# Last layer of a perceiver stack: four tiles in step, against two pairs of tiles half a pass apart

## What the last layer computes

```python
h = x + attention(rmsnorm(x, ln1_w), ...)     # x: layer-normed stream
out = h + moe(rmsnorm(h, ln2_w), ...)
# in moe:
probs = jax.nn.sigmoid(x @ router_w + router_b)
scores, idx = jax.lax.top_k(probs, TOPK)
for e in range(NR):
    combined = combined + w[..., e:e + 1] * expert_ffn(x, r_gate[e], r_up[e], r_down[e])
# expert_ffn: (silu(x @ wg) * (x @ wu) / SCALING) @ wd
# stream: x = x + _L3_ffn_ref(_layernorm(x), ...)
```

## Time and profile before

| | us |
|---|---|
| median of 3 runs (lowest, highest) | 4422.85 (4418.86, 4425.76) |
| the profiled execution's own time | 4422.6 |
| its span, first to last instruction | 4420.8 |
| last layer: first instruction of pass 0 to last of pass 1 | 4100.65 to 4414.15 |
| its two passes | 157.25 and 156.25 |

### The profile page before, as it was taken

How to read it: one execution, slowest core, us unless ns; L and a number is a source line. 1 busy time by engine, 2 the same in 40 slices (tenths; PEclk the granted TensorE clock), 3 DMA queues, 4 the chain that set the end, 5 groups by cost and what they waited for, 6 DMA issues and landing times. The chain is left out here.

```text
span 4420.8 us, 69997 instructions
## 1 busy us (share of the span) xinstructions
PE 3591.5 (81%) x26672; PEld 2566.4 (58%) x26672; DVE 2633.6 (60%) x5418; ACT 1722.9 (39%) x3305; POOL 361.6 (8%) x566
## 2 busy tenths in 40 slices
PE   7999998997787887753888776878888886878778
PEld 4655557876764555531555643535555555757667
DVE  6888885443367777876444363247667665453552
ACT  4888883111344343421333212224444442223323
POOL 3000000000000000000111000111111111121000
PEclk8555558998886666756988788989999997989787
DMA  2000001000010000010000014000000001200000
GB/s 78 1 0 0 0 0 72 0 0 19 7 36 20 0 0 0 0 58 2 5 5 5 5 59 134 0 3 3 3 5 3 3 3 35 82 0 0 1 1 10
DMA packets 44826, 72.66 MB, mean 16 GB/s; under 512 B 25805, under 2 KB 33489, under 8 KB 41045
## 3 DMA queue, kind: packets, MB, share of 16 engines
q1 hardware_dynamic: 36440, 70.54, 4.6%
q10 hardware_dynamic: 8256, 0.52, 0.2%
HBM read 67.91 MB, written 3.15 MB: 16 GB/s over the span
## 5 line engine op out<-in xcount | busy, mean ns | idle before, releaser
L1316 DVE TENSOR_SCALAR_CACHE_REDUCE l0x_ex<-l0x_s_ps 128x1024 f32<-128x1024 f32 x258 | 305.6, 1222 | 63.4 <-PE l0x_s_ps L1019 62.4
L1151 ACT ACTIVATE l0x_ex<-l0x_ex,l0x_neg_max,l0x_q_scale 128x2048 f32<-128x2048 f32 x128 | 267.9, 2093 | 52.4 <-DVE l0x_neg_max L1322 50.7
L1031 PEld LDWEIGHTS l0x_t_ps<-l0x_identb,l0x_pb 128*128 128x128 bf16 x2048 | 200.0, 142 | 109.4 <-issue 56.8
L1019 PE MATMUL l0x_s_ps<-l0x_kT,l0x_qT 64*128 64x512 bf16 x516 | 235.5, 600 | 32.9 <-ACT l0x_qT L1146 19.5
L1158 ACT ACTIVATE l0x_pt<-l0x_t_ps 128x1024 bf16<-128x1024 bf16 x256 | 246.3, 1014 | 32.2 <-PE l0x_t_ps L1031 32.2
L1031 PE MATMUL l0x_t_ps<-l0x_identb,l0x_pb 128*128 128x128 bf16 x2048 | 233.7, 304 | 6.8 <-ACT l0x_pt L1158 4.1
L1331 DVE TENSOR_SCALAR l0x_pb<-l0x_ex 128x2048 bf16<-128x2048 f32 x128 | 156.4, 1222 | 0.0
L263 PE MATMUL l3x_bank<-l3x_wproj,l3x_cat 128*128 128x256 f32 x512 | 120.7, 390 | 32.1 <-DVE l3x_cat L3345 32.1
L263 PE MATMUL l3x_bank<-l3x_w_kv_x,l3x_ctxT 128*128 128x512 f32 x256 | 129.8, 655 | 0.9 <-ACT l3x_ctx_q L762 0.9
L263 PEld LDWEIGHTS l3x_bank<-l3x_wproj,l3x_cat 128*128 128x128 f32 x512 | 96.1, 193 | 52.4 <-DVE l3x_cat L3345 38.7
L1019 PEld LDWEIGHTS l0x_s_ps<-l0x_kT,l0x_qT 64*128 64x128 bf16 x516 | 50.0, 121 | 129.4 <-issue 80.4
(11 more groups left out here) (740 smaller groups left out, 8651.6 us busy)
## 6 DMA issues: line engine op xcount, KB each, us to landing
l3x_wproj<-in_L_xattn_wproj SPq DMA_DIRECT2D x1, 4096.0 KB, 22.5
l3a_w<-in_L_attn_W SPq DMA_DIRECT2D x4, 1024.0 KB, 11.4
l2f_w<-in_L_ffn_w SPq DMA_DIRECT2D x1, 2816.0 KB, 12.4
l0x_ctxT<-in_ctxT SPq DMA_DIRECT2D x8, 256.0 KB, 3.0
l0a_wq<-in_L_attn_W_Q SPq DMA_DIRECT2D x1, 2048.0 KB
l0a_wk<-in_L_attn_W_K SPq DMA_DIRECT2D x1, 2048.0 KB
l0a_wv<-in_L_attn_W_V SPq DMA_DIRECT2D x1, 2048.0 KB, 8.0
l0a_wo<-in_L_attn_W_O SPq DMA_DIRECT2D x1, 2048.0 KB, 13.0
```

The costliest lines, as they stand in the source:

```text
L1019: ins = mm(s_ps[:, j * 512:(j + 1) * 512], qT[rows, h // 2, :], kT[rows, h // 2, j * 512:(j + 1) * 512], start=True, stop=True)
L1031: ins = nc.tensor.transpose(t_ps[:, j * P:(j + 1) * P], pb[:, h % 2, j * P:(j + 1) * P], identb[:])
L1151: s.activation(ex[:, h % 4, :], ex[:, h % 4, :], ACT.Exp, scale=q_scale[:, h:h + 1], bias=nb[:, h:h + 1], accum_out=sums[:, h:h + 1]).then ...
L1316: v.tensor_scalar(ex[:, h % 4, c], s_ps[:, c], 1.0, None, ALU.mult, ALU.max, accum_out=mx[:, h, half:half + 1]).then_inc(o.up(scores_taken ...
```

## The change

Within the pairs (0, 1) and (2, 3) the ways stay in step. The pairs are 16 steps apart: way n waits `16 * (n // 2)` empty steps in the order in which instructions are written. The loop over passes is unrolled, in Python: each way writes pass 1 directly behind its pass 0. The order has 80 rounds where there were 2 times 32: rounds 0 to 15 hold steps 0 to 15 of the first pair alone; rounds 16 to 63 hold, in each round, a step of the attention half of one pair and of the expert half of the other; rounds 64 to 79 hold steps 16 to 31 of the second pair alone. In a round the instructions of ways 0 and 1 stand before those of ways 2 and 3. `t` is now a number and no register.

```diff
                 pe.wait_ge(lat_v_ready.sem, lat_v_ready.value(t, 2))
-                pe.sem_inc(order["pe"], 1)
                 for i in range(H):
...
+        def in_its_turn(n, program, eng):
+            yield from steps(16 * (n // 2))
+            for t in range(TILES // WAYS):
+                yield from program(eng, t)
+
...
             pe.wait_ge(env.own.sem, env.own.value())
-            with pe.Fori(0, TILES // WAYS) as t:
-                in_turn(*(tile["tensor"](pe, t) for tile in tiles))
+            in_turn(*(in_its_turn(n, tile["tensor"], pe) for n, tile in enumerate(tiles)))
...
-            with act.Fori(0, TILES // WAYS) as t:
-                in_turn(*(tile["scalar"](act, t) for tile in tiles))
+            in_turn(*(in_its_turn(n, tile["scalar"], act) for n, tile in enumerate(tiles)))
...
-            with pool.Fori(0, TILES // WAYS) as t:
-                in_turn(*(tile["gpsimd"](pool, t) for tile in tiles))
+            in_turn(*(in_its_turn(n, tile["gpsimd"], pool) for n, tile in enumerate(tiles)))
...
-            with dve.Fori(0, TILES // WAYS) as t:
-                in_turn(*(tile["vector"](dve, t) for tile in tiles))
+            in_turn(*(in_its_turn(n, tile["vector"], dve) for n, tile in enumerate(tiles)))
```

## The result

| | before | after |
|---|---|---|
| median of 5 runs (lowest, highest), us | 4424.14 (4418.86, 4429.39) | 4442.77 (4434.28, 4449.16) |
| ratio, 95% interval | 1 | 1.0039 [1.0023, 1.0056] |
| profiled execution: time, span | 4422.6, 4420.8 | 4437.45, 4435.7 |
| last layer, from its first instruction to its last | 313.50 | 333.11 |

The change costs 0.4%, 18.6 us of the median.

What follows compares the result with a forecast made beforehand. No one engine bounds the layer throughout: DVE in rotations and softmax, PE in the experts. 66.1 + 3 x 81.0 + 28.0 = 337.1 us against 313.5, 23.6 more, gave 4446 us, range 4420 to 4468.

Steps and rivals of the forecast that it cites:

- F: Rounds 0 to 15, first pair's attention half alone: 63.7 us plus 2.4 for ACT's clearing and table load, 66.1.
- H: Each of three half passes with overlap: 63.7 us for attention plus 17.3 inserted by the other pair's experts, 81.0.
- D: Rounds 64 to 79, second pair's experts alone: seven at 3.4 us, plus 4.2 for the ends, 28.0.
- a pair alone is no half of four: Attention half: two tiles take over half of four's time, as other tiles no longer cover the engine chain; 63.7 us.
- The no-change point of H: Length of an overlapped half pass at which the layer would stay at 313.5 us: 73.1 us.
- 3.9 in round 3: Expert products inserted before the queries in an overlapped half pass: 2.6 to 5.2 us, taken as 3.9.
- from round 11 on I had 5.8: Late inserts in an overlapped half pass: 3.2 us in round 11, 1.3 in round 13, 1.3 in round 15.
- 2.0 for the scores behind the transpose: Round 6: scores wait behind an expert transpose whose gates stand behind DVE's rotations; 0 to 4.4 us, taken 2.0.
- 1.8 for the table load: Round 7 of an overlapped half pass: ACT's table back and two Silu add 1.8 us.
- That is where the expected gain goes: Rounds 4 to 7: 20 us of DVE work beside only two experts, where PE could do seven.
- PE does little: Expected sign: some 20 us per overlapped half pass of DVE rotating and shifting, PE's granted clock well under 1.00.
- rival 1: Whole layer faster: halves fill each other, PE stays at 1.00; half pass 71 us, layer 303, time 4412; chance 0.08.

Runs made afterwards that it cites:

- off64: Changed kernel with the pairs 64 steps apart instead of 16, so they never overlap; single run 4482.06 us, layer 374.17 us.
- hollow: Changed kernel without experts 1 to 6, their steps left empty, experts 0 and 7 kept; single run 4384.27 us, layer 282.27 us.
- attfirst: Changed kernel with the pair in its attention half written first in every round; 4444.05 us, ratio 1.0050.
- nosilu: Changed kernel with Silu replaced by Copy, leaving 8 of 15 table loads; 4445.24 us, ratio 1.0048.
- stretch: Changed kernel with 20 attention steps, offset 20, each tile's rotation and softmax cut over 7 steps, Exp behind both; 4447.74 us, ratio 1.0062.
- stretch2: Changed kernel with 20 attention steps, offset 20, tiles whole, the pair's odd tile in rounds of its own; 4448.79 us, ratio 1.0064.
- ahead: Unrolled kernel, all four tiles in step, with the second pass's norms set among the first pass's experts; 4409.52 us, ratio 0.9975 against the kernel before.
- warm: Changed kernel with ten unread products before PE's waits in rounds 6 and 8 of each overlapped half pass; 4441.93 us, ratio 1.0040.

## Why the prediction was right, and where its steps were off

**The sum.** Term by term, the layer's five stretches:

| | forecast | measured |
|---|---|---|
| F | 66.1 | 67.95 |
| H, mean of three | 81.0 | 78.6 (79.15, 79.87, 76.80) |
| D | 28.0 | 29.34 |
| layer | 337.1 | 333.1 |
| time | 4446, range 4420 to 4468 | 4442.8 |

**That a pair alone is no half of four** was the step that decided, and it is shown: F is 67.95 with nothing beside it, H without six experts is 68.3, and off64 prices pairs without overlap at 61.3 us. The no-change point of H was put at 73.1; with the measured F and D it is 72.1, and H was 78.6.

**Some luck in the sum.** That it came within 4 us owes something to errors that cancel. I gave F 2.4 us for ACT's clearing; the latent projection begins 7.8 us in, in F, and 6.9 in hollow's H, so it was 0.9. That makes the pair's own chain 67.95 - 0.9, some 67, against my 63.7: the values product took 10.6 (4136.66 to 4147.24) where I had 9.3, the way from its end to the router 8.5 where I had 7.5, and the rest lies before. The inserts were too large by more: 78.6 less 67 is under 12, against my 17.3.

**What the experts insert** was mis-sized. H less F was to be 81.0 - 66.1 = 14.9 and is 78.6 - 67.95 = 10.7. Its single entries were worse than their sum. The early rounds of the first H cost 7.6 by the latent projection, where I had 3.9 in round 3 and nothing for the norm behind the gates on DVE; from round 11 on I had 5.8, and the first H lost nothing more there (11.7 behind hollow where the values product begins, 11.2 at its end). Of the 2.0 for the scores behind the transpose and the 1.8 for the table load, attfirst and nosilu won nothing back that shows. A list of inserts by round is good for a total, not for places: attfirst takes 7 us of stalls out, and the total stays.

**"That is where the expected gain goes"**, the two experts in four long rounds, is the step that fell, most plainly by hollow: with only two experts left an H still takes 68.3 us, so all that any placing of the other six could win is 10.3 an H, and 6.5 of it are needed to break even. stretch and stretch2 won none of it, though each had a cost of its own. (By the prediction's own terms DVE's work in rounds 4 to 7 is 9.7 + 8.2 = 17.9 us, not 20.) The gain goes to the chain. In the orders tried here no H was shorter than one pair's own way from engine to engine, 66.6 to 68.4 us.

**Table loads.** The count of 15 was right; the 1.8 us in round 7 don't show: nosilu won nothing by taking that load away. The Trainium skill, "ScalarE: Activation LUTs", section "What ACT_TABLE_LOAD costs", adds a drain of some 1.38 us to each load. The trace doesn't agree: the routing's first DVE operation came 1.61 us after the load began, and the 1.28 us of the load and the sigmoid's 0.31 fill that time.

**The clock.** I had said that the layer's granted clock would be no higher than 0.78. Over the whole layer it is 0.80, and within the H 0.82 and 0.83, against 0.71 to 0.75 in hollow's: experts beside the attention half do keep it up, more than I allowed. In the stretch from the rotations to the values product (4182.92 to 4213.90) PE was busy for 24.1 of 31.0 us at 0.83; "PE does little" was wrong. That is rival 1's mechanism, present but too small: the H needed to fall by another 6.5 us to break even. The Trainium skill, "Perfetto Trace Analysis", section "Optimization Strategy", says that interleaving regimes with different busiest engines may improve performance. Half a pass of offset doesn't bear it out here, since the interleaving was paid for with the four tiles' cover; ahead does, with 0.25%.

**D.** Two tiles' experts follow each other by 3.33 us, against 3.4 in the sum (the list of what the profile should show said 2.6, which contradicted the sum and was wrong). Timeline of PE after, last stretch:

```profile
4417.29 1.12 PE L263 MATMUL l3f_bank<-l3f_w_in,l3f_rms_yT 128*128 128x256 f32 x4
...
4420.62 1.12 PE L263 MATMUL l3f_bank<-l3f_w_in,l3f_rms_yT 128*128 128x256 f32 x4
```

The 1.3 us by which D was under-sized most likely come from its start: up to 4407.27 the granted clock was 0.53, and the first expert's two products took 2.07 and 1.91 us, where later ones took 1.12 and 1.03.

**What stays open:** which waits set the length of an H once one of them is taken away (the total of the insert was measured, its places move with the order), the rest of the 8 to 12 us between the two orders in stretch2, and whether rounds of more equal length would pay without the added table loads and without the cutting.

## What to carry to other kernels

Before ways that run in step are split into groups, run one group alone: here its length was about the floor of every overlapped stretch. Two tiles alone took 68 us for the attention half, and as much with two of the other pair's experts beside it, where four in step pay 60 for each two with the same two experts. Overlap between groups must win back that price and the filling and emptying at both ends before it wins anything. To fill an idle stretch of one engine, move only the other engine's work that the next pass allows early, and keep the ways in step.

## What the runs showed of the chip that I had not expected

- PE's granted clock was mostly won at one product and lost at a later one. With ten extra products, 2.40 us, in front of PE's wait before them the scores ran at 1.00 (3.95 us, against 6.17 at 0.60), and the values product of 17 columns, on which PE was busy throughout, ran at 0.62 (11.19 us, against 9.02 at 0.78). The same pairs stand in the other traces: over the twelve H of after, attfirst, nosilu and warm, the values product was granted 0.78 or 0.79 in the three where the scores had 0.60, and 0.61 to 0.67 in eight of the nine where they had 1.00. The ninth, warm's second H, had 1.00 and 0.81.
- A program that is unrolled from a loop of two passes ran as fast as the loop: 0.9999 [0.9990, 1.0008].
- Seven table loads of 1.28 us fewer in the layer made no difference that the runs can tell: 1.0048 [1.0031, 1.0065] against 1.0039 [1.0023, 1.0056]. Where a load stands between ready data and the instruction that needs it, as in stretch2's first H, ACT goes from the load straight to the `Exp` (4211.38, 1.28 us, then 4212.67).
